# Local attention on one core: scores and key projection in one piece each, a split of the weights on another engine, and the mask as eight small products

## The reference

```
for i in range(6):                                   # 16 heads of 64, window 32
    q, k, v = split(shift_tokens(x) @ Wqkv[i])
    q = rotary(l2norm(q) * q_scale[i]);  k = rotary_inverse(l2norm(k) * k_scale[i])
    sim = q_window @ [k_previous_window, k_window]^T * 8
    sim = where(mask, -max, sim)                      # 32 queries see 64 keys, a band of it
    x = softmax(sim) @ [v_previous_window, v_window] @ Wo[i] + x
    a, gate = split(layernorm(shift_tokens(x)) * g + b) @ W1[i] + b1[i])
    x = (a * gelu(gate)) @ W2[i] + b2[i] + x
```

## Time and profile before

| | before |
|---|---|
| median of 3 runs | 1665.17 us (1661.12 to 1668.48) |
| profiled execution | 1664.71 us, span from first to last instruction 1662.6 us |
| TensorE clock granted | 0.999 |
| busy: PE, PEld | 1603.9 us (96%), 1226.0 us (74%) |
| busy: DVE, ACT, POOL | 1352.6 us (81%), 1178.3 us (71%), 1305.1 us (78%) |
| chain that ended last | PE 60%, SPq 16%, DVE 11%, POOL 6%, issue 5%, ACT 2% |

### The profile page before, as it was taken

The page is one execution under the profiler, slowest core; times in us unless marked ns, Lnnn a source line. Parts: engine busy times, 40 slices in busy tenths (PEclk is TensorE's granted clock), DMA queues, the critical chain, the costliest instruction groups (busy, mean ns, idle before and its releaser), DMA issues.

```text
span 1662.6 us, 70904 instructions
## 1 busy us (share of the span) xinstructions
PE 1603.9 (96%) x29520; PEld 1226.0 (74%) x29520; DVE 1352.6 (81%) x1879; ACT 1178.3 (71%) x1784; POOL 1305.1 (78%) x1257
## 2 busy tenths in 40 slices
PE   8999989999999999999999999999999999999998
PEld 5777866667677777777777777776777777777777
DVE  6677867888788888788888788888788888888886
ACT  5788846677677677677677767767777776776774
POOL 6423158888888898888899888889888998888884
PEclk9999999999999999999999999999999999999999
DMA  6211113433333443334343334343334433333333
GB/s 173 59 43 41 51 27 92 113 84 98 96 76 92 106 101 92 92 90 107 84 99 89 88 93 110 86 104 85 87 93 112 97 95 90 83 75 82 80 83 75
DMA packets 128205, 146.42 MB, mean 88 GB/s; under 512 B 58256, under 2 KB 71312, under 8 KB 127120
## 3 DMA queue, kind: packets, MB, share of 16 engines
q1 hardware_dynamic: 127296, 141.43, 34.7%
q10 hardware_dynamic: 592, 0.46, 0.1%
HBM read 25.43 MB, written 1.05 MB: 16 GB/s over the span
## 4 chain that ended last, share of the span: by engine, by line
PE 60%; SPq 16%; DVE 11%; POOL 6%; issue 5%; ACT 2%; DMA 0%; POOLq 0%; DVEq 0%; ACTq 0%
PE banks L1474 37%; SPq L454 12%; PE banks L1734 6%; PE banks L1781 6%; PE banks L1851 5%; PE banks L1624 4%; DVE small L1296 1%; POOL arena L675 1%; DVE arena L1249 1%; DVE small L1278 1%; DVE arena L1244 1%; DVE small L1272 1%; POOL arena L726 1%; POOL arena L720 1%; DVE small L1284 1%
## 5 line engine op out<-in xcount | busy, mean ns | idle before, releaser
L670 POOL TENSOR_TENSOR arena<-arena 128x1024 f32<-128x1024 f32 x96 | 230.3, 2399 | 49.6 <-DVE arena L1249 44.5
L1296 DVE TENSOR_REDUCE small<-banks 128x16 f32<-128x1024 f32 x96 | 117.5, 1224 | 181.5 <-PE banks L1781 180.1
L954 ACT ACTIVATE vst<-banks 128x1024 f32<-128x1024 f32 x192 | 196.5, 1023 | 87.9 <-PE banks L1474 58.0
L1244 DVE TENSOR_TENSOR arena<-banks,tabs 128x1024 f32<-128x1024 f32 x192 | 233.4, 1215 | 3.5 <-ACT arena L910 3.5
L1249 DVE TENSOR_TENSOR arena<-banks,tabs 128x1024 f32<-128x1024 f32 x192 | 233.3, 1215 | 0.0
L675 POOL TENSOR_TENSOR arena<-arena 128x1024 f32<-128x1024 f32 x96 | 229.0, 2386 | 0.0
L665 POOL TENSOR_TENSOR prob<-prob,small 128x1024 f32<-128x1024 f32 x95 | 182.4, 1920 | 19.1 <-DVE small L1286 18.5
L720 POOL TENSOR_TENSOR arena<-arena,small 128x1024 f32<-128x1024 f32 x96 | 186.2, 1940 | 7.5
L726 POOL TENSOR_TENSOR arena<-arena,small 128x1024 f32<-128x1024 f32 x96 | 183.0, 1906 | 9.2
L1851 PE MATMUL banks<-arena 128*32 128x128 f32 x6144 | 188.5, 274 | 1.5 <-issue 1.0
L1474 PE MATMUL banks<-qkH,xsH 128*128 128x512 f32 x384 | 175.2, 456 | 9.8 <-DVE arena L1249 4.4
(11 more groups left out here) (197 smaller groups left out, 3717.2 us busy)
## 6 DMA issues: line engine op xcount, KB each, us to landing
arena<-vst SPq DMA_DIRECT2D x1536, 64.0 KB, 2.0
qkraw<-in_wqk_dram SPq DMA_DIRECT2D x11, 512.0 KB
arena<-in_wvo_dram SPq DMA_DIRECT2D x5, 1024.0 KB
tabs<-in_tab_dram SPq DMA_DIRECT2D x40, 128.0 KB, 2.6
gq<-w1w SPq DMA_DIRECT2D x58, 64.0 KB, 2.0
MH<-w1w SPq DMA_DIRECT2D x56, 64.0 KB, 2.0
lns<-Xt SPq DMA_DIRECT2D x94, 32.0 KB
lns<-Xt SPq DMA_DIRECT2D x94, 31.8 KB
```

Source lines behind the costliest of these rows:

```text
L670: pool.tensor_tensor(kc, kc, ks, ALU.add).then_inc(s["k_add"], 1)
L954: act.activation(vst[:, g, :], two(V_BANK), ACT.Copy).then_inc(s[f"v_cp{g}"], 1)
L1244: dve.tensor_tensor(heads(c), heads(two(0)), table(k % NT, kind), ALU.mult).then_inc(s[done], 1)
```

## The change

- In TensorE's list the fourth part of the scores follows the third directly, and both halves of the key projection stand together behind them.
- `up_gate(.., 0)` and `next_shifts` are moved ahead of `transpose_probs`.
- The mask is issued as eight products of 64 rows, 32 columns and 512 elements (four groups of 32 queries, two row halves) instead of two of 128 columns; its constants `maskR` and `pickR` are bf16 and the masked value becomes -2^100, which bf16 holds exactly.
- The subtraction for the lower query weights of layers 1 to 5 moves from GpSimd to VectorE, where it stands ahead of the maxima in the step at place 0.

```diff
-        maskR = sb("maskR", [P, 2 * WIN], F32R)
-        pickR = sb("pickR", [P, 2, NW, WIN], F32R)
+        maskR = sb("maskR", [P, 2 * WIN], BF16)
+        pickR = sb("pickR", [P, 2, NW, WIN], BF16)
...
 (GpSimd's loop)
-                next_query_weights(G - 1)
...
 (VectorE)
+            def next_query_lower(k):
+                if is_tile(k) and k % TILES == TILES - 1 and k < LAST_TILE:
+                    dve.wait_ge(s["wq_H"], k // TILES + 2)
+                    dve.tensor_tensor(query_L, qkraw[:, :], query_H, ALU.subtract).then_inc(s["wq_L"], 1)
...
                 next_folded_upper(G - 2)
+                next_query_lower(G - 1)
                 maxima(G - 2)
...
 (TensorE, masked)
-                for o in range(2):
-                    r = slice(64 * o, 64 * o + 64)
-                    mask = maskR[r, :].rearrange("p (e k) -> p e k", e=1).to_broadcast([64, NP, 2 * WIN])
-                    mm(bk(4 + o).rearrange("p (j k) -> p j k", j=NP), pickR[r, first, :, :].rearrange("p w c -> p (w c)"), mask)
+                for w in range(NW):
+                    for o in range(2):
+                        r = slice(64 * o, 64 * o + 64)
+                        mask = maskR[r, :].rearrange("p (e k) -> p e k", e=1).to_broadcast([64, NP, 2 * WIN])
+                        mm(bk(4 + o)[WIN * w:WIN * (w + 1), :].rearrange("p (j k) -> p j k", j=NP), pickR[r, first, w, :], mask)
...
 (TensorE's loop)
                 up_value(chunk_at(G, 11), 0)
+                up_gate(chunk_at(G, 10), 0)
+                next_shifts(chunk_at(G, 12))
                 transpose_probs(G - 3)
-                up_gate(chunk_at(G, 10), 0)
                 scores_a(G - 2)
                 scores_b(G - 2)
                 next_products_upper(G - 2)
                 scores_c(G - 2)
-                if G:
-                    project_keys_first(G)
-                next_shifts(chunk_at(G, 12))
                 scores_d(G - 2)
                 layer_columns(chunk_at(G, 13))
                 if G:
+                    project_keys_first(G)
                     project_keys_last(G)
```

More of the change, by code:

```diff
@@ L43 @@
 NC = B * T // CH
-NEG = -1.0e30
+NEG = -2.0 ** 100
 C_SH, C_ID, C_LAST, C_CAUS, C_1, C_MASK = 0, 1, 128, 160, 288, 289
@@ L574, in lower_key_weights, with first_query_weights @@
                 pool.tensor_tensor(key_L[l % 2], qkraw[:, :], key_H[l % 2], ALU.subtract).then_inc(s["wk_L"], 1)
-            def lower_query_weights(l):
-                pool.wait_ge(s["wq_H"], l + 1)
-                pool.tensor_tensor(query_L, qkraw[:, :] if l else query_raw0, query_H, ALU.subtract).then_inc(s["wq_L"], 1)
+            def first_query_weights():
+                pool.wait_ge(s["wq_H"], 1)
+                pool.tensor_tensor(query_L, query_raw0, query_H, ALU.subtract).then_inc(s["wq_L"], 1)
             for n in range(NT // 2):
@@ L586, in _ @@
             rounded(query_raw0, query_H, "wq_H")
-            lower_query_weights(0)
+            first_query_weights()
             pool.wait_ge(s["wq_L"], 1)
@@ L737, in next_key_weights @@
                     lower_key_weights(k // TILES + 1)
-            def next_query_weights(k):
-                if is_tile(k) and k % TILES == TILES - 1 and k < LAST_TILE:
-                    lower_query_weights(k // TILES + 1)
             def shifted_lower(c):
```

## The result

The changed kernel takes 1718.63 us (median of 4 runs, 1704.8 to 1718.94) against 1665.89 us before (4 runs beside it): a ratio of 1.0286, 95% interval 1.0249 to 1.0322. The forecast was 1653 us and its range ended at 1669, so both the sign and the range missed. The profiled execution took 1718.62 us.

What follows compares the result with a forecast made beforehand. TensorE was taken to bind about half the steps, GpSimd and SyncE's queue the rest. Gains less 14.0 us of stalls summed to -12.4 us against the profiled 1664.7: 1652.3, stated as 1653 us, range 1630 to 1669.

Steps and rivals of the forecast that it cites:

- What bounds the kernel: TensorE binds half of layers 1 to 4, layer 5 and layer 0's last six steps; elsewhere GpSimd and SyncE's queue.
- TensorE-bound: Places 1 to 8 of layers 1 to 4, where TensorE is busy 115.8 of 116.9 us; 53 such steps overall.
- Scores and keys in one piece: Score run and key products on TensorE: 3.24 us becomes 3.00, saving 0.24 us a step, bounds 0.15 and 0.35.
- The mask: Eight overlapping mask products on TensorE: 0.05 us a step better, bounds 0.15 better to 0.6 worse.
- The stall: Bias products ahead of the softmax weights wait for h2: five places at 2.8 us, 14.0 us lost.
- Lower query weights: Subtraction moved to VectorE at layer starts: gains 1.4 us in layers 3 and 4, 0.4 in layers 1 and 2.
- the 6.0 us of that line of the sum: Gain at places 9 to 0: 1.0 us each in layers 1 and 2, 2.0 each in layers 3 and 4.
- Gate products first: Gate products ahead of softmax weights save a tile-shape change: 0.07 us a step, plus 0.3 us in four waits.
- Rival 2: SyncE's transfer queue pins the second half and part of the first, stalls eat the rest: 1661 us; chance 0.22.
- Rival 3: The eight mask products do not overlap, 0.74 us more per TensorE-bound step: 1692 us; chance 0.14 with other losses.

Runs made afterwards that it cites:

- e11: Kernel after with the mask again as two float32r products and the bias products back between the key halves: 1653.80 us, ratio 0.9938 to before.
- e4: Kernel before with only the scores and keys in one piece, bias products behind the first key half: 1661.74 us, ratio 0.9958.
- the three pairs: Three pairs of kernels differing only in whether the bias products stand behind the first key half: 1.24, 1.40 and 1.53 points of the ratio.
- e6: Kernel before with only the lower query weights moved from GpSimd to VectorE: 1663.98 us, ratio 0.9997.
- e5: Kernel before with the mask's part of the change alone (eight bf16 products, -2^100): 1693.29 us, ratio 1.0164.
- e10: Kernel after with its mask again as two products in float32r: 1681.32 us, ratio 1.0091 to before.

## Why the forecast was wrong, step by step

- **What bounds the kernel** fits what the clean kernel e11 shows. Time of eight steps each, in one profiled execution per kernel, from score run to score run, from the first tile on (us); the odd columns are the halves called TensorE-bound:

```
steps     0-8   8-16 16-24 24-32 32-40 40-48 48-56 56-64 64-72 72-80 80-88
before  112.4  122.1 116.8 121.2 116.3 120.6 116.1 120.0 116.2 118.8 116.0
e11     112.0  120.6 113.6 120.4 113.1 121.5 114.8 120.6 113.9 121.5 116.0
after   116.6  125.1 124.4 121.7 126.4 121.7 125.8 121.7 123.7 122.0 118.8
```

  In e11 the TensorE-bound halves of layers 1 to 4 get 3.2, 3.2, 1.3 and 2.3 us shorter (forecast 2.9 with the mask, 2.5 without it), the others between 1.5 shorter and 2.7 longer: what TensorE saves there does not come through, as the forecast had it. In after it is the same TensorE-bound halves that get 7.5 to 10 us longer, the others 0.5 to 3.2.
- **Scores and keys in one piece:** 0.11 us measured over all steps without a gap, 0.25 in those without a pause either, 0.24 forecast with 0.15 as the lower bound. The forecast priced a record at 10 ns from step 41, which was a fast one: over the first 96 score records the median of the kernel before is 11 ns, and in e4 it is 11 ns too. In the clean steps the run takes 1.53 us to the first wide product and the keys 1.59 (forecast 1.42 and 1.58).
- **The mask:** its block is 0.06 us shorter, 0.05 forecast. The step that failed is that I priced the six added products by what they take on the array. I reckoned 12 records more at nothing, named the Trainium skill's overhead per product as the one charge against them and set it aside with the 10 ns records. That very rate is the trouble: 16 + 256 records of mask and scores in 0.23 + 1.53 us are more than one packet. **No term of the sum was for the supply of instructions:** 42.7 us more of missing instructions in the trace of after, and 32 us of time for the mask.
- **The stall:** 13.8 us in five waits of up to 3.1, 14.0 forecast; the places were right too. What failed is its price: I took a wait of 2.8 us to cost 2.8 us. By the three pairs the five cost 21 to 25 us; the rest fits the half clock around them. **No term was for the clock.** The rows had it at 1.00 in both halves of layer 2, and I did not ask what an idle stretch longer than any in that trace would do.
- **Lower query weights:** the 6.0 us of that line of the sum are 3.6 for the waits at layer starts and 2.4 for what the shorter steps save in those halves. The 3.6 are what e6 tests; it measured 0.03%, 0.5 us, at most 2.7 by its interval. The wait has another name afterwards. The step that failed took the releaser of a wait for its only cause.
- **Gate products first:** 2.3 us by the ratio, not distinguishable from nothing; 0.07 us a step was forecast.
- **Rivals.** Rival 2's sign, over 40 us of waits of the values' copy for its transfers, is there (44.2, had 21.4), and in e11 TensorE's wait for that copy is its largest. Rival 3 had the right edit, the right sign and, at 27 us, by chance e5's size; its mechanism, column groups in series, is refuted by the shorter block. Its chance of 0.14 was too small because it stood for one mechanism only.

One path through the runs adds up to the whole (ratios, in us; the forecast's terms in brackets): the change without mask and stall, e11, -10 (-24); the stall, e11 to e10, +25 (+14); the mask, e10 to after, +32 (-3). That makes +48 (-12). So the sign was lost to the mask and the stall, and the savings too were less than half of what was reckoned. By another order of the same parts the shares shift: put into the kernel before alone, the mask costs 27 us.

How well do the other terms hold by themselves? For e11, which has neither the mask nor the stall, they give -12.4 - 14.0 + 53 x 0.05 = -23.8 us; it measured -11.5. The missing 12 can be made up of the query waits (3.6), 3.9 us more of gaps than before, and of clock (17.1 - 3.4) / 2 = 6.9 at most. The merge's 0.11 us instead of 0.24 would be another such part; which of them it is, no run shows.

What stays open: where in a packet the request for the next one is made. In after the next packet's transfer began 1.07 us (median) after the first of the 256, and no gap ended less than 2.23 us after that start, but the trace does not show the request. Whether more records or smaller tiles of the mask bring the gaps was not parted by a run. And the summed losses of after (88 us) exceed the growth of its span (54) by more than e11's gain of 11.5 accounts for; that other engines catch up behind the gaps is a guess, not shown by a run.

## What to carry to other kernels

Count TensorE's instructions where small tiles stand in a row, not only their time: a product and its weight load are two, and here a packet of 256 that was used up in under 8 us could be followed by a gap, one that took longer never was. When such a run is there, a product more is not free because the array overlaps it: here two wide mask products, with the change of tile shape that they cost, were worth 32 us over eight small ones. Wide work between the small is no such sure gain: parting the scores gained 0.3 to 0.4% with the eight mask products, which the intervals do not tell from nothing, and cost 0.4% without them. And price a new wait on TensorE with the clock around it: here 2.8 us of wait cost 4 to 5.

## What the runs showed of the hardware that was not expected

- **The length of a gap goes with the data transfers.** Of the 281 gaps in the fourteen traces, 10 had the DMA engines over 80% busy with data on average over 1 us on either side of their start and were 3.18 us long on average (up to 4.83); 71 gaps with under 20% were 0.88 us (up to 1.87). In the worst case above SyncE had just issued the eight transfers of the values. The DMA line of after from 306 to 313 us, in 40 slices:

```profile
DMA  9699899999347999999999669431211111115401
```

  The gap began at 307.5, and the packet's transfer only 2.2 us later, when the row falls: instructions seem to wait for the same DMA engines as the data.
- **A boundary between packets is not always hidden.** Of the 1333 boundaries in the table above, 281 have a gap. The Trainium skill, "Runtime: NRT & Kernel Launch", section "Instruction fetch mechanics", says that instructions come in blocks of 256 while the one before is executed; the packets and the remainder 193 agree. It adds that the cost of a boundary is "mostly hidden", which holds here for the 683 behind slow packets and not for those 281.
- **The rate of a run of small products differs from step to step:** the first 96 score records of the kernel before take 0.92 us in the fastest step and 1.05 at the median, 9.7 and 11 ns a record; one step does not give the price.
- **The clock falls within a stall or up to 2.6 us behind it, and stays low after it.** TensorE stood still from 1066.4 to 1069.1; the granted clock fell at 1068.45, before work resumed, and rose at 1075.28. At another of the five stalls work resumed at 574.3 and the clock fell at 576.9.
